# The end of a fused layer kernel on one core: guard columns collected, spread and judged ahead of the last root, and the last unit's output summed on two engines and stored per tile

## The reference

```
a   = softmax_causal(Q K^T / sqrt(32) - (i - j)) V        # 16 heads of 32, from LN(x)
x1  = x + LN(a Wo^T + bo)
h   = LN(x1) @ Hadamard(512)                              # then 4-bit levels per row
z   = quantize(h) @ ternary(W_ffn)^T
out = x1 + LN(z)
```

## Time and profile before

| what | us |
|---|---|
| median of 3 runs | 1270.02 |
| lowest and highest of them | 1265.23 and 1274.75 |
| the profiled execution: its own time | 1269.99 |
| its span in the profile | 1268.3 |
| busy in the span: TensorE, VectorE, ScalarE, GpSimd | 1130.2, 998.5, 669.0, 558.0 |

### The profile page before, as it was taken

The page is one execution under the profiler, slowest core; times in us unless marked ns, Lnnn a source line. Parts: engine busy times, 40 slices in busy tenths (PEclk is TensorE's granted clock), DMA queues, the critical chain, the costliest instruction groups (busy, mean ns, idle before and its releaser), DMA issues.

```text
span 1268.3 us, 44027 instructions
## 1 busy us (share of the span) xinstructions
PE 1130.2 (89%) x18337; PEld 744.0 (59%) x18368; DVE 998.5 (79%) x2424; ACT 669.0 (53%) x1427; POOL 558.0 (44%) x715
## 2 busy tenths in 40 slices
PE   2789999999999989999999999999999999999751
PEld 1566666665566666656666665666666656666420
DVE  2776788888877888887888888888888888887782
ACT  3444556545555555555556555555565555554431
POOL 0234345454444545444455454444544544444332
PEclk9899999999999999999999999999999999999885
DMA  6764665767666567665675877566577665655431
GB/s 181 182 141 108 123 132 136 144 156 137 126 137 129 134 145 156 134 131 134 138 139 135 156 152 130 132 138 133 132 146 157 145 140 133 138 124 117 107 75 43
DMA packets 241549, 170.39 MB, mean 134 GB/s; under 512 B 186913, under 2 KB 187425, under 8 KB 241249
## 3 DMA queue, kind: packets, MB, share of 16 engines
q1 hardware_dynamic: 236656, 150.48, 56.8%
q0 software_dynamic: 4688, 17.04, 4.5%
HBM read 41.09 MB, written 16.78 MB: 46 GB/s over the span
## 4 chain that ended last, share of the span: by engine, by line
PE 55%; SPq 16%; issue 7%; ACT 7%; DMA 7%; DVE 6%; POOL 1%; POOLq 0%; ACTq 0%; DVEq 0%
PE f_job L1160 35%; SPq L322 13%; DMA f_stacks<-f_stage 5%; PE f_o L1272 4%; PE f_job L1299 3%; PE f_o L1277 3%; PE f_st L1252 3%; PE f_job L1232 3%; PE f_job L1220 2%; ACT f_PT L577 2%; SPq L307 2%; ACT f_xin L538 1%; ACT f_x2h L610 1%; PE f_job L1309 1%; DMA f_xin<-x 1%
## 5 line engine op out<-in xcount | busy, mean ns | idle before, releaser
L435 POOL TENSOR_SCALAR_AFFINE_SELECT f_PT<-f_PT 64x512 f32<-64x512 f32 (+1 forms) x256 | 170.1, 685 | 426.2 <-ACT f_PT L577 313.5
L450 POOL TENSOR_TENSOR f_square<-f_stage 128x512 bf16<-128x512 f16 x128 | 132.3, 1053 | 116.0 <-ACT f_stage L555 116.0
L577 ACT ACTIVATE f_PT<-f_st 128x512 f32<-128x512 f32 x192 | 106.8, 601 | 133.0 <-PE f_st L1252 133.0
L1160 PE MATMUL f_job<-f_xTh,f_wqh 128*128 128x256 f16 x512 | 142.2, 278 | 24.4 <-DVE f_wkl L743 24.4
L555 ACT ACTIVATE f_stage<-f_job,f_bias 128x256 f16<-128x256 f32 x256 | 106.3, 467 | 95.0 <-PE f_job L1160 93.1
L842 DVE SCALAR_TENSOR_TENSOR f_stage<-f_job,f_bias,f_stage 128x256 f16<-128x256 f32 x256 | 110.6, 475 | 48.1 <-ACT f_stage L555 48.1
L1160 PE MATMUL f_job<-f_xTh,f_wql 128*128 128x256 f16 x512 | 141.5, 276 | 1.7 <-issue 1.7
L1160 PE MATMUL f_job<-f_xTl,f_wqh 128*128 128x256 f16 x512 | 141.3, 276 | 0.4 <-issue 0.4
L1160 PE MATMUL f_job<-f_xTh,f_wkh 128*128 128x256 f16 x512 | 140.2, 274 | 0.8 <-issue 0.8
L1160 PE MATMUL f_job<-f_xTl,f_wkh 128*128 128x256 f16 x512 | 140.2, 274 | 0.6 <-issue 0.6
L1160 PE MATMUL f_job<-f_xTh,f_wkl 128*128 128x256 f16 x512 | 140.1, 274 | 0.0
(11 more groups left out here) (152 smaller groups left out, 2915.6 us busy)
## 6 DMA issues: line engine op xcount, KB each, us to landing
f_stacks<-f_stage SPq DMA_DIRECT2D x384, 128.0 KB
f_xin<-x SPq DMA_DIRECT2D x32, 512.0 KB, 5.0
f_x<-x SPq DMA_DIRECT2D x32, 512.0 KB, 4.5
out<-f_z POOLq DMA_DIRECT2D x32, 512.0 KB, 4.4
f_Vmix<-f_V SPq DMA_DIRECT2D x32, 256.0 KB
f_Vmix<-f_V SPq DMA_DIRECT2D x64, 128.0 KB
f_stacks<-rows_const SPq DMA_DIRECT2D x3, 512.0 KB, 6.9
f_stacks<-wqT SPq DMA_DIRECT2D x1, 1024.0 KB, 8.3
```

The costliest lines, as they stand in the source:

```text
L435: nc.gpsimd.affine_select(out=d, in_=d, compare_op=ALU.is_ge, fill=0.0, base=odd * SUB, pattern=[[0, 4], [0, TP], [1, SUB]], channel_multi ...
L450: nc.gpsimd.tensor_tensor(square[:, 2 * m + pair, :], h, h, ALU.mult).then_inc(squared, 1)
L577: nc.scalar.activation(dst, src, ACT.Exp, scale=1.0 / SS).then_inc(expd, 1)
L1160: mm = pe.matmul(dst, lhs[a](c), rhs[b](c), start=(n == 0), stop=(n == 3 * KC - 1))
```

## The change

Nothing ahead of the end is touched. In the end:

- VectorE collects the guard columns right behind `x_stats(last)`, ahead of `z_columns(last - 1)`, and judges them behind `find_scale(last, 1)`, ahead of `scale_out(last, 0)`.
- GpSimd does the all-reduce behind `finish_out(last - 1)`, ahead of `z_root(last)`.
- Of the last unit's output GpSimd sums tile 0 alone (`finish_first`) and VectorE tile 1, as its last instruction (`finish_second`, which waits until both tiles are normalised).
- SyncE stores the two tiles by a DMA of 256 KB each, each when its tile is summed (`store_tile`). GpSimd waits for these two and for the 31 DMAs of the other units.

```diff
+            def store_tile(k, t, made):
+                sp.wait_ge(made, 1)
+                sp.dma_start(rows_of(out, k)[:, t, :], z[:, t, :]).then_inc(last_done, 16)
...
             turn_q(last, 1)
+            store_tile(last, 0, first_made)
+            store_tile(last, 1, second_made)
...
+            def spread_guard():
+                pool.wait_ge(guard_step, 8)
+                nc.gpsimd.partition_all_reduce(guard2[:], guard[:], P, bass.bass_isa.ReduceOp.max)\
+                  .then_inc(guard_spread, 1)
+
+            def finish_first(k):
+                pool.wait_ge(z_normed, TP * k + 1)
+                nc.gpsimd.tensor_tensor(z[:, 0, :], z[:, 0, :], x1[k % 2][:, 0, :], ALU.add).then_inc(first_made, 1)
...
             finish_out(last - 1)
+            spread_guard()
             z_root(last)
-            finish_out(last)
-
-            pool.wait_ge(guard_step, 8)
-            nc.gpsimd.partition_all_reduce(guard2[:], guard[:], P, bass.bass_isa.ReduceOp.max)\
-              .then_inc(guard_spread, 1)
-            pool.wait_ge(out_done, 16 * STEPS)
+            finish_first(last)
+
+            pool.wait_ge(out_done, 16 * (STEPS - 1))
+            pool.wait_ge(last_done, 16 * TP)
...
+            def finish_second(k):
+                dve.wait_ge(z_normed, TP * k + TP)
+                nc.vector.tensor_tensor(z[:, 1, :], z[:, 1, :], x1[k % 2][:, 1, :], ALU.add).then_inc(second_made, 1)
...
             x_stats(last)
+            collect_guard()
             z_columns(last - 1)
             find_scale(last, 0)
             find_scale(last, 1)
+            judge_guard()
             scale_out(last, 0)
             scale_out(last, 1)
             z_stats(last)
             z_columns(last)
-
-            (the guard's instructions, L1107 to L1130)
+            finish_second(last)
```

More of the change, by code:

```diff
@@ L229, in fast_path @@
         out_done = sem("out_done")
+        first_made = sem("first_made")
+        last_done = sem("last_done")
+        second_made = sem("second_made")
         guard_step = sem("guard_step")
@@ L915, in residual, with judged, collect_guard @@
                 note(nc.vector.scalar_tensor_tensor(y_off[k % 2], y_mv[:, :, 0], -1.0, y_rstd, ALU.mult, ALU.mult))
+            gs = [0]
+            def judged(ins):
+                gs[0] += 1
+                ins.then_inc(guard_step, 1)
+                dve.wait_ge(guard_step, gs[0])
+            def collect_guard():
+                dve.wait_ge(norms_kept, STEPS)
+                for i in range(2):
+                    rows = slice(i * 64, (i + 1) * 64)
+                    judged(nc.vector.tensor_reduce(guard[rows, 6 + i:7 + i], nmax[rows, :], AX_X, ALU.max))
+                dve.wait_ge(min_found, STEPS)
+                judged(nc.vector.tensor_reduce(guard[:, 8:9], mmin[:], AX_X, ALU.min))
+                judged(nc.vector.tensor_scalar(guard[:, 8:9], guard[:, 8:9], -1.0, None, ALU.mult))
+                dve.wait_ge(x_stats_made, TP * STEPS)
+                judged(nc.vector.tensor_reduce(guard[:, 9:10], x_mv[:, :, :, 0], AX_XY, ALU.max,
+                                               apply_absolute_value=True))
+                judged(nc.vector.tensor_reduce(guard[:, 10:11], x_mv[:, :, :, 1], AX_XY, ALU.max))
+                judged(nc.vector.tensor_reduce(guard[:, 11:12], x_mv[:, :, :, 1], AX_XY, ALU.min))
+                judged(nc.vector.tensor_scalar(guard[:, 11:12], guard[:, 11:12], -1.0, None, ALU.mult))
@@ new lines, in judge_guard @@
+            def judge_guard():
+                dve.wait_ge(guard_spread, 1)
+                g1, passed = guard2[0:1, :], guard[0:1, :]
+                judged(nc.vector.tensor_scalar(passed[:, 0:4], g1[:, 0:4], WSPAN[1], None, ALU.is_le))
+                judged(nc.vector.tensor_scalar(passed[:, 4:8], g1[:, 0:4], WSPAN[0], None, ALU.is_ge))
+                judged(nc.vector.tensor_scalar(passed[:, 8:10], g1[:, 4:6], BMAX, None, ALU.is_le))
+                judged(nc.vector.tensor_tensor(g1[:, 12:13], g1[:, 6:7], g1[:, 7:8], ALU.mult))
+                judged(nc.vector.tensor_scalar(passed[:, 10:11], g1[:, 12:13], (SPAN * SS) ** 2, None, ALU.is_le))
+                judged(nc.vector.tensor_scalar(passed[:, 11:12], g1[:, 8:9], DEPTH * SS, None, ALU.is_le))
+                judged(nc.vector.tensor_scalar(passed[:, 12:13], g1[:, 9:10], MEAN, None, ALU.is_le))
+                judged(nc.vector.tensor_scalar(passed[:, 13:14], g1[:, 10:11], VARIANCE[1], None, ALU.is_le))
+                judged(nc.vector.tensor_scalar(passed[:, 14:15], g1[:, 11:12], -VARIANCE[0], None, ALU.is_le))
+                judged(nc.vector.tensor_reduce(g1[:, 0:1], passed[:, 0:15], AX_X, ALU.min))
+                judged(nc.vector.tensor_scalar(flag_sb[:], g1[:, 0:1], -1.0, 1.0, ALU.mult, ALU.add))
@@ L1094, in _ @@
             z_columns(last)
[L1097 to L1128, removed]
@@ L1129, in _ @@
-            judged(nc.vector.tensor_reduce(g1[:, 0:1], passed[:, 0:15], AX_X, ALU.min))
-            judged(nc.vector.tensor_scalar(flag_sb[:], g1[:, 0:1], -1.0, 1.0, ALU.mult, ALU.add))
+            finish_second(last)
         @block.tensor
```

## The result

The changed kernel took 1261.29 us (median of 6 runs, 1258.73 to 1262.68) against 1267.88 (6 runs, 1265.23 to 1274.75): a ratio of 0.9943, 95% interval 0.9921 to 0.9966. It is faster by 0.6%, and its slowest run lies under the fastest one of before. The profiled execution took 1262.68 us, its span 1261.1.

A forecast was written before the change was run, and what follows sets the result against it. It took the end as a chain of single steps handed between engines. Root at 1257.5, landed 1264.3, drained 1264.5 against 1263.77 before gave + 0.7 us on 1270.02, so 1270.7 us; range 1265.5 to 1276.9.

The forecast's parts named there:

- The collecting: Eight VectorE instructions ahead of `z_columns(last - 1)`: 1.77 us with the hand-over, putting `norm_z(last - 1)` that much later.
- The spreading: GpSimd's all-reduce in its new place: configuration at 1242.92, 5.69 us to the all-reduce, which runs 1248.61 to 1249.00.
- The judging: Eleven VectorE instructions, 1.96 us, ahead of `scale_out(last, 0)`; VectorE waits until 1249.10 and hands over 5.3 us later.
- The change back: GpSimd reloads TENSOR_TENSOR's set before the last root: 5.69 us from 1251.79, putting the root 8.4 us later, at 1257.5.
- rival C: GpSimd's drain is slow by itself, whatever the last work: A's times plus 2.8 us, 1270.6; chance 0.43 together with the forecast.
- The end of the last unit: Split sums and two stores: all landed at root + 6.8 us against + 8.0 before, giving back 1.2 us.
- The drain: GpSimd's drain at the end, behind a plain sum long done, takes 0.2 us.
- A: Rival: the tail isn't GpSimd's all-reduce work, so the change back starts at 1249.00: - 2.1 us, 1267.9; chance 0.27.
- VectorE's first judging step: Sign of being right: in the last unit it waits some 5 us for the all-reduce, near 1249.
- E: Rival: the change works as meant, VectorE never stalls, the root comes at 1250.4: - 6.4 us; chance 0.02.
- D: Rival: the first change, to the all-reduce's set, too takes 11.9 us: + 10 to + 13 us; chance 0.03.
- B: Rival: the change back is as long as the one at the start, 11.9 us: 1274.1 to 1276.9 us; chance 0.25.

The follow-up runs named there:

- E1: The kernel before, with one small TENSOR_TENSOR added as GpSimd's last operation, behind the all-reduce: 1273.37 us, ratio 0.9983 to the kernel before.
- e2: The changed kernel, with a second all-reduce of a tile of zeros as GpSimd's last operation: 1277.14 us, ratio 1.0035 to the kernel before.
- e4: The changed kernel with collecting, all-reduce and judging back at the end, leaving only the split output: 1269.76 us, ratio 0.997 to the kernel before.
- e5: The changed kernel, with the waits for all output DMAs moved from GpSimd to SyncE: 1265.06 us, ratio 0.9911 to the kernel before.

## Why the prediction was wrong

**The step that failed** stands in its first paragraph: the change "acts only on the last 32 us". The sum had no term for the start, and the start gave 7.5 us, more than the whole gain of 6.6. The rows that should have raised the question were on the table: the chain itself has 7.83 us of "issue" ahead of the first root. I read from rows 6 that 11.9 us passed ahead of the first TENSOR_TENSOR, wrote that the input explained only the first four, and used it as a price for the end. I never asked why a change was needed there at all, with nothing but fills and one DMA of GpSimd's ahead of it, nor what it cost where it stood. E1, e2 and e4 showed the answer: it follows from what the execution before left behind.

**The collecting** was right: `norm_z(last - 1)` was put 1.62 us behind the last Hadamard product and came at 1.65.

**The spreading** was right: 5.69 us expected from configuration to all-reduce, 5.67 of idle time measured; the all-reduce was put 12.0 us behind the Hadamard product and came at 11.7.

**The judging** was right: `scale_out` was put 14.4 us behind and came at 14.2.

**The change back** was there, and held the root as said, but two terms were mis-sized against each other. It took 6.94 us and not 5.69 (a row that I had called quiet, though the output's 512 KB moved beside its first 2 us), and it began at the all-reduce's end and not 2.79 us behind. The root came 19.1 us behind the Hadamard product, not 20.9. Over six kernels the change back took 6.94 to 7.66 us in quiet. The 2.79 us of the drain were not the all-reduce's: e5's drain ended 2.7 us behind a plain sum, and the changed kernel's lasted 2.68 with GpSimd idle for 3.6 us before it. That is rival C, which I had joined to the forecast for its time. With its change back 1.2 us longer, C is what the end did.

**The end of the last unit** was right as a sum: root + 6.8 us, expected and measured (1246.90 to 1253.7). Within it VectorE's sum took 1.15 us and not 0.69, beside GpSimd's own, and the stores landed in 2.4 to 2.6 and not 3.0.

**The drain** was put at 0.2 us and took 2.7. With the root 1.8 us too late and the drain 2.5 too short, the end came out at + 0.7 against + 1.6 measured: that it came so near is luck, two errors of opposite sign. By the end alone the kernel would be 1.6 us slower.

**The signs.** The configuration on the line of the last unit's root came. The gap from the all-reduce's end to the root was 6.94 us, between A's 5.7 and the forecast's 8.5. The long drain with no all-reduce ahead of it, named as a sign of being wrong, came too. VectorE's first judging step waited 8.16 us and not "some 5": that sign took the delay of 5.3 us for the wait, which by the prediction's own times is over 8.

**The rivals.** E's time, - 6.4 us, is the measured gain, but its mechanism is not: VectorE did stall, and the end got slower. (At - 6.4 us it doesn't move the time by over 6.9 either, as the prediction says of it; only D does.) A had the right start of the change back and B the right direction of its length, neither the time. No rival looked at the start. The chance of 0.95 for within 1% held; the range did not, as it was built from the end alone.

## What to carry to other kernels

Measure a change to the end of a kernel from a mark ahead of it, and compare the stretches: here the span fell by 7 us while the edited part grew by 1.6. Where an engine shows an unexplained wait at its first operation, ask what the program's last operation leaves it with, since the next execution starts from there. An all-reduce over partitions on GpSimd costs its set of operations twice, and here a transpose and a reduction on engines that stood idle were worth more than any place tried for it.

## What the runs showed of the hardware

- GpSimd's set of operations outlasts an execution. A configuration for the set in place costs nothing visible (6.5 against 14.3 us for the first root); what a first execution after another program pays was not tried.
- A change takes 5.6 to 6.4 us to the all-reduce's set, 6.9 to 7.7 back to TENSOR_TENSOR's in quiet, and 10.3 to 12.6 beside the loads at the start. The Trainium skill, "GPSIMD Engine Reference", section 2.1, gives some 6 us for the first call into a freshly loaded set: the trace agrees for the first kind, and the other two are longer.
- GpSimd's drain at the end takes 2.7 to 2.8 us behind its last work or its own start, whatever that work was (a sum in e5, an all-reduce in e4), against 0.17 at the start of the program. What it does in that time stays open; with the waits for the stores on SyncE it is hidden (e5: the meeting 0.3 us behind the landing, and not 3.0).
